# Zero products ahead of the first scan and past the last one, and a new order of all five engines, in a two-layer macaron block

## The reference

```python
x = x + 0.5 * L0_ffn(layernorm(x))    # rows quantised to blocks of 16 on an FP4 grid, gate/up to 704, silu, down
x = x + L0_attn(layernorm(x))         # Mamba: W_in, convolution of 4 taps, silu, W_x, W_dt, softplus,
                                      #   scan over 512 positions of 512 channels x 16 states, gate silu(z), W_out
x = x + 0.5 * L0_ffn(layernorm(x))
x = x + 0.5 * L1_ffn(layernorm(x))    # base linear map plus 8 gated LoRA experts
x = x + L1_attn(layernorm(x))         # 16 heads of 16 channels, causal, ALiBi bias
x = x + 0.5 * L1_ffn(layernorm(x))
```

## Time and profile before

| | us |
|---|---|
| median of 3 runs | 4607.52 (4603.06 to 4627.58) |
| the profiled execution | 4599.0 |
| its span, first to last instruction | 4597.2 |
| mean granted TensorE clock | 0.944 |

### The profile page before, as it was taken

How to read it: one execution, slowest core, us unless ns; L and a number is a source line. 1 busy time by engine, 2 the same in 40 slices (tenths; PEclk the granted TensorE clock), 3 DMA queues, 4 the chain that set the end, 5 groups by cost and what they waited for, 6 DMA issues and landing times.

```text
span 4597.2 us, 55200 instructions
## 1 busy us (share of the span) xinstructions
PE 3972.7 (86%) x18768; PEld 2065.4 (45%) x18799; DVE 3997.4 (87%) x5964; ACT 2376.6 (52%) x4341; POOL 1639.1 (36%) x1037
## 2 busy tenths in 40 slices
PE   4677788898999899989989999889888888988977
PEld 2233344444545354444535444444544444444443
DVE  6698989998999999899998989899898999988622
ACT  2443454655565555646546465555546554555433
POOL 1153533343434334333433334343443343334100
PEclk9789999999999999999989999999999999999987
DMA  1587886877777787777876876787787787678200
GB/s 60 149 199 188 178 207 146 203 149 186 174 169 191 158 202 168 187 165 176 194 168 172 175 182 161 168 209 160 183 187 180 148 189 177 140 200 184 69 31 23
DMA packets 241438, 753.48 MB, mean 164 GB/s; under 512 B 37650, under 2 KB 132659, under 8 KB 171524
## 3 DMA queue, kind: packets, MB, share of 16 engines
q1 hardware_dynamic: 241156, 749.95, 70.0%
HBM read 647.30 MB, written 101.71 MB: 163 GB/s over the span
## 4 chain that ended last, share of the span: by engine, by line
DVE 41%; PE 31%; DMA 10%; issue 7%; ACT 6%; POOL 2%; SPq 2%; DVEq 0%; ACTq 0%; POOLq 0%
DVE state L1689 12%; DVE u L1684 6%; DVE mt L1786 6%; DMA state<-dtx_scratch 5%; PE m L1178 4%; PE m L1205 3%; PE pd L1399 3%; PE y L1267 2%; PE y L1279 2%; PE m L1220 2%; DVE front L1594 2%; DMA decay<-dt_scratch 2%; DVE front L1623 2%; DVE front L1598 2%; POOL state L784 1%
## 5 line engine op out<-in xcount | busy, mean ns | idle before, releaser
L784 POOL TENSOR_TENSOR state<-state,bc 128x1024 f32<-128x1024 f32 x512 | 1243.7, 2430 | 1606.9 <-DVE u L1684 1604.7
L1689 DVE TENSOR_TENSOR_SCAN state<-decay,u 128x1024 f32<-128x1024 f32 x512 | 1167.1, 2279 | 9.0 <-ACT decay L979 0.6
L979 ACT ACTIVATE decay<-decay,a_neg 128x511 f32<-128x511 f32 x1024 | 675.4, 713 | 219.7 <-DMA decay<-dt_scratch 219.1
L1178 PE MATMUL m<-w_gu,hats_m 128*128 128x480 f32 (+1 forms) x1536 | 710.0, 583 | 60.0 <-DVE front L1598 41.1
L1684 DVE TENSOR_TENSOR u<-state,bc 128x1024 f32<-128x1024 f32 x512 | 649.4, 1268 | 52.9 <-DMA state<-dtx_scratch 41.0
L1267 PE MATMUL y<-state,sel 128*32 128x512 f32 x2048 | 295.1, 652 | 150.3 <-POOL state L784 149.5
L765 POOL TENSOR_TENSOR front<-front,hsc_m 128x704 f32<-128x704 f32 x128 | 189.5, 1481 | 641.6 <-DVE front L1503 641.6
L1178 PEld LDWEIGHTS m<-w_gu,hats_m 128*128 128x128 f32 x1536 | 268.5, 193 | 327.8 <-issue 159.1
L1205 PE MATMUL m<-w_dn,front 128*128 128x256 f32 x1536 | 385.5, 393 | 16.8 <-ACT front L912 16.5
L1125 PE MATMUL y<-minus,zero 128*128 128x512 bf16 x1290 | 334.2, 384 | 0.0
L1205 PEld LDWEIGHTS m<-w_dn,front 128*128 128x128 f32 x1536 | 286.6, 194 | 103.2 <-ACT front L912 51.2
(11 more groups left out here) (263 smaller groups left out, 7163.3 us busy)
## 6 DMA issues: line engine op xcount, KB each, us to landing
decay<-dt_scratch SPq DMA_DIRECT2D x256, 1024.0 KB, 7.4
state<-dtx_scratch SPq DMA_DIRECT2D x256, 1024.0 KB, 11.6
qk_scratch<-shared SPq DMA_DIRECT2D x64, 384.0 KB, 6.0
shared<-qk_scratch SPq DMA_DIRECT2D x384, 64.0 KB
kh<-qk_scratch SPq DMA_DIRECT2D x384, 64.0 KB
xs_scratch<-front SPq DMA_DIRECT2D x16, 1024.0 KB, 12.7
dt_scratch<-front SPq DMA_DIRECT2D x256, 64.0 KB, 3.6
dtx_scratch<-hats_m SPq DMA_DIRECT2D x256, 64.0 KB, 4.2
```

The costliest lines, as they stand in the source:

```text
L784: eng.tensor_tensor(st, st, bc[:, 1:2, :].to_broadcast([P, WIDE, L]), ALU.mult).then_inc(scan_pool.sem, scan_pool.step(f"c{r}{h}"))
L979: ins = eng.activation(d, d, ACT.Exp, scale=a_neg[:, g:g + 1])
L1178: mm = eng.matmul(f.bank(f"gu{t}{p}")[:, 0:2 * width], norm.hat_t[:, k, t * P:(t + 1) * P], w_gu[:, k, 2 * lo:2 * (lo + width)], start=(k ...
L1689: eng.tensor_tensor_scan(st, decay[:, n % ND, h * WIDE * L:(h + 1) * WIDE * L], u[:, :], 0.0, ALU.mult, ALU.add).then_inc(scan_dve.sem, sc ...
```

## The change

Four edits in the code, and new strings.

- `mine` starts with `"y": True`, so digits 5 may stand from the end of the set-up on.
- After the last step of `scan(15)` one more step on TensorE waits for ScalarE's read of `Y` (`res1`), issues one product of zeros with `start=True` into `Y`, and sets `mine["y"]`, so that digits 5 may stand to the end of the program.
- On ScalarE the first hat of an item p of `WORK` waits, where item p-2 is an FFN, for that FFN's transposes (`x1`).
- All five strings are new. SP, POOL, ACT and DVE hold the same number of each digit as before. PE has one more 1 and 1690 digits 5 in place of 1347.

```diff
@@ lead, ScalarE
                     if p >= 2 and WORK[p - 2][0] == "head":
                         for saved in dtx_saved:
                             eng.wait_ge(saved, 128 * (WORK[p - 2][1] + 1))
+                    elif p >= 2:
+                        eng.wait_ge(f.pe.sem, f.pe.after(FFNS.index(WORK[p - 2]), "x1"))
@@ TensorE
-            mine = {"y": False, "pd": False}
+            mine = {"y": True, "pd": False}
@@ scan, TensorE
                     mm.then_inc(scan_pe.sem, scan_pe.step(f"o{t}"))
+                if i == B - 1:
+                    yield
+                    eng.wait_ge(scan_act.sem, scan_act.after(i, "res1"))
+                    eng.matmul(Y[:, 0:P], zero16[:, :], minus16[:, :], start=True, stop=True)
+                    mine["y"] = True
@@ ORDER["PE"], first lines
-        "00000000000000440444000004404440000044444444440000000000000000000000000015555550055000055555555555555555555555515500550000555"
...
+        "55555555555555555550055000000000055555555555555500455404440000045540440444000004554544455555445544455555555555555555555500005500"
...
@@ ORDER["DVE"], first lines
-        "33333333333333330000000000000000000000000000000000000000000000000000333333333333333333333000000000000000033300000000000000000010"
-        "00011111110011100100000000010100000110000000101000001100000001101000110000000001010111133333333113333333311011101101100000110110"
...
+        "33333333333333330000000000000000000000000000000000000000000000000000333333333333333330000000030300000003333300000000000000000010"
+        "10001111110011010010000000010100000110001010010100010010100010010101010001000001010010100111133133133333331331331311010130010133"
...
```

More of the change, by code:

```diff
@@ L81 @@
[L81 to L88, removed]
@@ new lines @@
+        "22121122222222222212211222222222222122112222221110011000000000000100001111100000000000000001001121001101111111112211222222222222"
+        "22222222122212222222111222222222222222222221122222222222222111122222211100110000000011100000000111000000001000000001001100112110"
+        "11111112211222222222222222222222222222222112221222112222222222222211222222222222221122222211111011000000000000100000111110000000"
+        "00000000000110011211011111112211222222222222222222222222222111222122211122211222222222222221122222222222222112222221110011000000"
@@ new lines @@
+        "00000100000111110000000000000000101011020110111111122112222222222222222222222222222112211222111222122222222222222122222222222222"
+        "11112222221110011000000000000100010111100000000000000000101112001101111111221111222222222222222222222222222222112221112222222222"
+        "22222221122211222222222221122222211101100000000000001000110111000000000000000001011102011011111112211222222221122222222222222222"
+        "12122221111222122222222222222222111122222222222222111222112220000000000000010101001110000000010000000000111001121101111122111122"
@@ new lines @@
+        "22222222222222222222222222221122212221122222222222222112222222222222211222112221110110000000000000100010111100000000000000000010"
+        "01112110111111122112222222222222222222222222222221111222222111222222222222221122222222222222111122222211111000000000000001110000"
+        "11110000000020000000000110001111122111112222222222222222112222222222222211112222221112222222222222211122221222222222211222222011"
+        "11100000000011111100000000111200000000000000000010011011111112211222211222222222222222222222222221111122211222112222222222222211"
@@ new lines @@
+        "22222222222222111222222110000000000000011100001110000000000000010000111200110111111122112222222222222222222222222222212111222111"
+        "22222222222222222112222221212222222112222221110110000000001000000001111100000000000000001101201110011111112211222222222222222222"
+        "22222222221221112222222222222212222221122222222222222112222221111111110020000000000010010010111000000000000000010022111002222222"
+        "22222222222222222222221211122211222222222222222221112222222222222211222112221111111111121111122222222222222222222222222222222222"
@@ new lines @@
+        "33330000333333331111110111011110110111333313331311111111111133331111101101110110113333110333310111101101111122221111333312222111"
+        "10111011011101133133010133313101011111111111222222223333111111101022212110101113333103133301011101111111111122221333312221211101"
+        "10110222210113333113333010110110111111111122221122223333111101110122221011101113333333301101111001111111111122222222133331111011"
+        "01222211011011133330333310111011011111111111222222223333111111101022221101011333313333101011011101111111111122222222333311111011"
@@ new lines @@
+        "22220110110111110133330111011333130111111111222233331112222111010122221010111333311011010333131101111111111122223331312222101101"
+        "12222011101113333113333001110111011111111111222222223333111222121011011101110133331010111033133101111111111122222222333311111101"
+        "22220111011011133331333310101111010111111111222222221331331111012222101101011133331010313331101101111111111122222222133313111112"
+        "22211010110101133330110110101111111122221111222222223333111111110111011011110111122221122212111112222111333300002222222222222222",
```

275 lines of the change are left out of this document (131 added, 144 removed).

## The result

| | before | changed |
|---|---|---|
| median of the runs, us | 4608.82 (4603.06 to 4627.58) | 4494.05 (4485.92 to 4506.54) |
| runs | 4 | 4 |
| profiled execution / its span | 4599.0 / 4597.2 | 4488.22 / 4486.4 |
| mean granted TensorE clock | 0.944 | 0.969 |
| VectorE busy, us | 3997.4 | 3905.1 |

The ratio is 0.9746, with a 95% interval of 0.9708 to 0.9784: faster by 115 us, where 63 were forecast and 4500 us was the low end of the range. The direction was right and the size was not.

The account below looks back on a forecast made before the run. VectorE's order was taken to bound the middle, latency and TensorE's clock the ends. From 4599 us, 25 for the ends and 35 for the middle came off; 8.5 added for the median gave 4547, rounded to 4545, range 4500 to 4608.

Parts of the forecast that it names:

- Clock at the start: Ahead of the first scan, added zero products hold TensorE's clock at 2.4 GHz: 8 us gained.
- Overrun of the 70: Ahead of the z projection, 70 zero products (15.4 us) outlast a 6.95 us wait: 1 us charged, at worst 8.5.
- Clock at the end: In the last loras and attention 15, zero products hold TensorE's clock: 9.6 us for two lora rounds, 1.9 and 4 for attention.
- a gain of 2 between -4 and +6: At the end, FFN 31 finishing inside attention 14 clears lora 29 but leaves the wait ahead unfilled: 2 us gained.
- The middle: Through the scans, 599 fewer close pairs free 72 us of VectorE's time; 35 us taken, bounds 0 and 66.
- The price of a close pair: On VectorE, a step waiting for the one directly ahead costs 0.12 us more than a pair without such a wait.
- The argument against, from the zero products of the middle: In scans 2 to 14, zero products fall only from 862 to 844, counted against a shorter period.
- The ends only: Rival: only the ends gain; in the middle, savings return as waits for TensorE: 4582.5 us, chance 0.20.
- All of it: Rival: ends gain 35 us and middle 66, as VectorE sets the pace wherever busy: 4506 us, chance 0.12.
- The slower one: Rival: half scans between the FFN quantisation's links make VectorE wait, half of 252 us exposed: 4637 us, chance 0.11.
- The clock was held: Denies the rival that the clock is not held or zero products outlast waits at the ends: 4591 us, chance 0.07.
- What would show it: Signs: clock near 0.95 at the ends, first multiply by B 8 us earlier, first scans 1 to 4 us closer.

Follow-up runs that it names:

- edits of its start: Changed kernel with ScalarE's exp moved back, zero products cut from 70 to 24, or a store put ahead of loads, in four combinations: 4499.06, 4498.2, 4482.7, 4497.67 us.
- the kernel with the near waits: Changed kernel, order kept, with 606 VectorE instructions each given a wait on the instruction directly ahead: 4553.79 us.
- the ends alone: Kernel before, all orders kept, with only the code edits and the 202 and 171 zero products added outside the scans: 4591.49 us.
- experiment 3: VectorE waits added, orders kept. Changed kernel: 606 on the instruction ahead 4553.79 us, 606 four back 4488.63, 1212 ahead 4623.89. Kernel before: 606 ahead 4673.29.
- all three edits of the start: Changed kernel with dt_scratch's eighth store ahead of the first loads, ScalarE's first decay exp behind ln3, and 24 zero products instead of 70: 4497.67 us.
- the other two of these edits alone: Changed kernel with ScalarE's first decay exp behind ln3 and 24 zero products instead of 70 ahead of the z projection: 4498.2 us.

## Why the prediction was wrong, step by step

- **Clock at the start: right.** It holds (0.94). The same instructions in the timeline of TensorE, to be laid beside the earlier trace rows:

```profile
83.86 1.77 PE L1183 MATMUL m<-w_gu,hats_m 128*128 128x448 f32 x4 [0.78 <-DVE front L1608]
...
114.31 2.86 PE L1210 MATMUL m<-w_dn,front 128*128 128x256 f32 x12 [0.37 <-ACT front L917]
...
125.86 3.70 PE L1225 MATMUL m<-hats_m,w_in 128*128 128x512 f32 x8 [0.42 <-ACT hats_m L856]
...
140.48 3.63 PE L1240 MATMUL m<-front,w_x 128*49 128x512 f32 x8 [1.11 <-DVE front L1639]
...
158.37 16.89 PE L1130 MATMUL y<-minus,zero 128*128 128x512 bf16 x70
```

  3.21 became 1.77, 5.17 became 2.86, 5.57 became 3.70 and 5.82 became 3.63: 7.8 us, 8 forecast, and 7.5 and 8.5 in two pairs of kernels.
- **Overrun of the 70, charged 1 us, at most 8.5: the wrong suspect.** They last 16.89 us, and the z projection starts behind them at 176.51 after a wait of 1.25 for VectorE, so they were over in time. The start did lose 5.7 us, 5.2 of them by the edit that I had put at nothing: "all DMAs keep their order but for some moved by a few places". I had asked only whether the load of the state is passed by a wait, not whether a small store is passed by large loads and who waits for its source.
- **Clock at the end: right for the single rows, too small in sum, and partly given back.** TensorE's timeline of `lora` 31, which answers to the earlier trace rows:

```profile
4460.01 5.34 PE L1130 MATMUL y<-minus,zero 128*128 128x512 bf16 x24
...
4468.53 1.96 PE L1303 MATMUL pg<-w_ra,hats_r 128*128 128x16 f32 x16 [0.31 <-ACT hats_r L856]
...
4474.33 1.99 PE L1317 MATMUL pd<-w_base,hats_r 128*128 128x256 f32 x4 [0.26 <-ACT shared L1002]
...
4481.78 0.59 PE L1320 MATMUL pu<-xx,ident 128*128 128x256 f32 x2
```

  The sixteen small products take 1.96 as forecast, the output tiles 4481.78 + 0.59 - 4474.33 = 8.0, not 7.2: the first of them still takes 1.99, the lower level's time, against 1.13 in the earlier trace rows. The zero products gave 25.9 us in this order, more than the 15.5 that I had for the clock, and the order's own tail cost 11.1, for which I had taken a gain of 2 between -4 and +6. Net 14.8.
- **The middle: the step that failed.** The price of a close pair was right (0.12 forecast, 0.117 measured at 606 places), and so was their number, 599. What failed is what I made of it: "Only what is not given back in VectorE's next wait counts", 35 us of 72, with 66 as the bound because VectorE is busy for 92% of the stretch. No such loss showed in the net: 606 closed pairs cost 71 us in the middle, 1212 cost 135, and in the old order 606 cost 77, with waits of 274 us in all on VectorE. 599 x 0.117 = 70 of the 93 us are this. Waits did give something back, but less than half: 17 of the 110 us that neighbours and durations saved from before to changed, and 20 of the 91 that the 606 added waits cost. What covered it was a term that I did not have, the durations of the same instructions. My reading of why so little came back is argued and not shown: VectorE's waits are for engines that wait for it in turn, so a chain that VectorE walks faster brings their answers sooner too. The share for which an engine is busy says nothing of it.
- **The rest of the middle, 22 us, was in no term.** With before's number of close pairs the changed order is still 22 us shorter there (4114.3 to 4092.0), and 21 of them are durations, since less time is lost to GpSimd's multiplies (88 against 68 us of stretch). One trace of each kernel stands behind this number. The middles of the changed kernel and of those with edits of its start range over 28 us (4016.0 to 4043.9), so its size is rough; by the medians the kernel with the near waits is 57 us under before's, of which its two ends have 19. With the multiply cut short the order kept 31 us of its own, in waits. Which engine's string brings it stays open: no run has one string of the new order among four of the old.
- **The argument against, from the zero products of the middle** (862 to 844, "where a shorter period with the same work on TensorE would leave it less to fill"), was none: their number is fixed by the string, whatever the period turns out to be, and TensorE's busy share of the stretch did rise, from 90.1 to 91.2%.
- **The rivals.** "The ends only", at 4582.5, is 9 us from what the ends alone measured (4591.49), but not what happened: the rule of the Trainium skill under it (VectorE: DVE Perf Modes, The DRAIN you can't avoid) does not hold for these neighbours, by experiment 3. "All of it", at 4506 and with a chance of 0.12, was the nearest, 12 us above the measured time, and that by luck: it had 35 us at the ends and 66 in the middle, where 18 and 93 were measured. The slower one did not come with this order, and did with neighbours exchanged on VectorE alone. The clock was held.
- **What would show it.** The spacing of first multiplies fell from 258.4 to 252.5 us, 5.9, where I had written 1 to 4. The chain of waits also shifted: where the earlier trace rows had VectorE at 41% and TensorE at 31%, the changed kernel's page has

```profile
PE 39%; DVE 34%; DMA 9%; ACT 7%; issue 7%; SPq 2%; POOL 1%; DVEq 0%; ACTq 0%; POOLq 0%
```

  and still 1212 more close pairs on VectorE cost nearly their full price. Here the share of an engine on the last chain was a poor measure of what its work is worth.

## What to carry to other kernels

In this kernel a cost spread between all instructions of the busiest engine counted nearly whole (71 us for 606 pairs), so don't discount one by the engine's idle share or by its share of the chain. That is no rule for every saving on that engine: 77 us of durations, saved where GpSimd's multiply had stretched 86 instructions, shortened the middle by 25. Price such a cost with the order standing still, by adding waits at many places and the same waits on something long over as control: exchanging steps moves other engines' inputs by far more than the cost itself. And when a queue's order changes, look at the small transfer that falls behind a large one, and at who overwrites its source.

## What the hardware showed that I had not expected

- A VectorE instruction that waits for its neighbour's end starts 0.034 us after it, one that does not starts 0.083 us before it (medians over the same 606 places of two kernels). The Trainium skill (VectorE: DVE Perf Modes, Two Vector instructions with no wait between them) says of instructions that it calls held that they start only when every earlier one has finished. It gives no price. The traces agree that others start before that, and show a wait on the neighbour to cost 0.11 us a pair in the total.
- GpSimd's multiply of 128x1024 holds some VectorE instructions that start while it runs until its own end: 0.19 us became 1.67 and at most 1.81 for one of 44 columns, which ended 0.04 to 0.05 us behind the multiply in all 26 cases where that had over 0.15 us to go, and a `u` of 1.23 us became 3.00 at most, ending 1.09 us behind the multiply. All stretches sum to 88 us over the kernel before, and to 15 us with the multiply cut short. The Trainium skill (SBUF — State Buffer, SBUF: two separate sides) has one pair of ports that VectorE and GpSimd share, held by either for a whole instruction; the end at 770.33 beside GpSimd's at 770.29 agrees with it.
- A store of 64 KB issued 1.92 us after a load of 1024 KB (159.43 and 161.35) let its waiter start at 172.28, and at 160.86 in the kernel with all three edits of the start, where it is issued ahead of it. With the other two of these edits alone the waiter starts at 172.11.
